# Attention block with a maximum brought in by a one-row product: the tile of that product, 64 rows against 32

## The chip, the cores and the metric

One core of a Trainium2 chip runs the whole program. The metric is the device time of one execution in microseconds. Five engines work beside each other and meet at semaphores: TensorE (PE, with its weight loads as PEld), VectorE (DVE), ScalarE (ACT), GpSimd (POOL) and SyncE (SP), which here issues the transfers.

## What is computed

The block takes `L0_attn_data`, 8 x 512 x 128 in float32, normalises each row, and returns the sum of three things: the input, a 16-head attention over the normalised rows, and a gated recurrence over them that ends in a tanh.

```
x = L0_attn_data                                   # (8, 512, 128)
xn = _layernorm(x, axis=-1)
# attention: 16 heads of 64
qkv = xn @ W_qkv + b_qkv
scores = jnp.einsum('nqhd,nkhd->nhqk', q, k)
attention = jax.nn.softmax(scores / jnp.sqrt(64.0), axis=3)
out = jnp.einsum('nhql,nlhd->nqhd', attention, v).reshape(n, l, 1024) @ W_out + b_out
# recurrence over the 8 entries of the first axis
ft = sigmoid(xt @ wf.T + c @ uf.T + bf); it = sigmoid(...); gt = tanh(...)
c = ft * c + it * gt
h = tanh(xn @ wo.T + c_final @ uo.T + bo)
return x + out + h
```

## The kernel before, in words

The work is written out by hand, one block of code for each engine, with semaphores between them; no scheduler reorders it. The outer loop runs over the 8 batches (the first and the last are written out, the six between are a loop), the loop inside over 4 steps `j` of a batch. A step handles two head pairs `t` and `t + 1`; there are 64 head pairs in all. A head pair is two heads of 64 features each, one in partitions 0 to 63 and one in partitions 64 to 127 (`OWN[0]` and `OWN[1]`).

For precision, queries and keys are split into a high and a low part (`QH`, `QL`, `KH`, `KL`), so a block of scores is the sum of three products. `scores` (line 786) makes the transposed scores of one block `u` of 128 keys against 512 queries for both heads, in PSUM tile `st[:, u % 2, h, :]`: line 796 accumulates KH·QH, KH·QL and KL·QH, each as a pair of products, one for each head, with 64 rows of the array each. The softmax needs the maximum of each query taken off before the exponential. `score_maxima` (line 770) computes rough scores the other way round in `mx`, VectorE reduces them to negated maxima (line 551, `NM`), `turn_max` (line 781) transposes them, and SyncE's transfers place them as single rows of `MROW` in partitions 0 and 64 (`AUX`, line 187). The fourth and last pair of `scores`, line 804, adds that row to every one of the 128 key rows: the stationary operand `ONEROW` has ones in partitions 0 and 64 and zeros elsewhere, and the moving operand `MROW` has the maxima there and zeros elsewhere (lines 236 to 241). This pair too is contracted over 64 rows for each head. The last product of the pair signals `st_done`, and ScalarE's exponential (line 387) takes the tile.

In between, the TensorE block issues other products in a fixed order: the next heads' projections (`pair_of_halves`, line 729, 64 rows each), the rough scores (line 777, 64 rows), the product of probabilities and values (line 812, 128 rows and 64 columns of the array), the sums of the probabilities (line 822, also 128 by 64), the output projection (line 828, 128 by 128), and in the first batch the projections of the first heads and the recurrence (lines 693 and 712, 128 by 128). How high a product's tile is follows from how many partitions its operands have, and where it stands from their first partition.

Of the kernel before, what the change touches and what calls it, by code (L numbers as in the profile page):

```python
# [5 lines left out]
def build_block(nc, data, W_qkv, b_qkv, W_out, b_out, wf, uf, bf, wi, ui, bi, wc, uc, bc, wo, uo, bo, in_c, out):  # L6
# [11 lines left out]
    HD = P // 2  # L18
# [7 lines left out]


    OWN = [slice(0, HD), slice(HD, P)]
    AUX = [slice(0, 1), slice(HD, HD + 1)]

    data_t = data.rearrange("n (b p) d -> p n b d", p=P)
# [4 lines left out]
    with ctx:  # L36
        def sb(name, shape, dt=f32):
            return ctx.enter_context(nc.sbuf_tensor(name, shape, dt))
# [22 lines left out]
        MROW = sb("MROW", [P, 2, L], f32r)  # L61
        ONEROW = sb("ONEROW", [P, P], f32r)
# [29 lines left out]
        st = ctx.enter_context(nc.psum_tensor("st", [P, 2, 2, L], f32))  # L92
# [53 lines left out]
        def wait(eng, s, value):  # L146

            if not (isinstance(value, int) and value <= 0):
                eng.wait_ge(s, value)

        def placed(n, j):

            return (STRETCHES * n + j + 1) * 32
# [11 lines left out]
        def _(sp):  # L165
# [16 lines left out]
            def place_max(n, j):  # L182
# [3 lines left out]
                for h in range(2):  # L186
                    sp.dma_start(MROW[AUX[h], :, :].bitcast(f32).rearrange("p a (b j) -> p (a b) j", j=P),
                                 TM[2 * TB * h:2 * TB * h + 2 * TB, :]).then_inc(d_m, 16)

            def place_first(a, copied, landed):  # L190
                sp.wait_ge(copied, 1)
                for h in range(2):
                    sp.dma_start(MROW[AUX[h], a, :].bitcast(f32).rearrange("p (b j) -> p b j", j=P),
                                 TM[2 * TB * h + TB * a:2 * TB * h + TB * (a + 1), :]).then_inc(landed, 16)
# [34 lines left out]
        def _(pool):  # L229
# [10 lines left out]
            for h in range(2):  # L240
                nc.gpsimd.memset(ONEROW[AUX[h], :].bitcast(f32), 1.0).then_inc(pads_set, 1)
                pool.wait_ge(pads_set, 3 + h)
# [446 lines left out]
        def _(pe):  # L689
# [32 lines left out]
            def pair_of_halves(groups, slots, halved, done):  # L722

                for slot in slots:
                    swap, i = slot // 3, slot % 3
                    for h in range(2):
                        dst, terms = groups[h ^ swap]
                        stationary, moving = terms[i]
                        last = nc.tensor.matmul(dst, stationary[OWN[h], :], moving[OWN[h], :], start=(slot == 0),  # L729
                                                stop=(slot == 5))  # L730
# [39 lines left out]
            def score_maxima(t, s, b):  # L770
# [5 lines left out]
                for h in range(2):  # L776
                    last = nc.tensor.matmul(mx[:, h, :], QH[OWN[h], s % 4, b * P:(b + 1) * P], KH[OWN[h], s % 4, :],  # L777
                                            start=True, stop=True)
# [7 lines left out]
            def scores(n, t, s, u, parts=range(4)):  # L786

                b = slice(u * P, (u + 1) * P)
                terms = ((KH, QH), (KH, QL), (KL, QH))
                if 0 in parts:  # L790
                    wait(pe, exp_done, 4 * t + u - 1)
                for i in parts:
                    if i < 3:
                        k, q = terms[i]
                        for h in range(2):
                            nc.tensor.matmul(st[:, u % 2, h, :], k[OWN[h], s % 4, b], q[OWN[h], s % 4, :],  # L796
                                             start=(i == 0), stop=False)
                    else:
                        if u == 0 and isinstance(n, int) and n == 0 and s < 2:
                            pe.wait_ge(d_m if s else d_first, 32)  # L800
                        elif u == 0 and s % 2 == 0:
                            pe.wait_ge(d_m, placed(n, s // 2))
                        for h in range(2):
                            last = nc.tensor.matmul(st[:, u % 2, h, :], ONEROW[OWN[h], :], MROW[OWN[h], s % 2, :],  # L804
                                                    start=False, stop=True)
                        last.then_inc(st_done, 1)

            def values(n, t, s, blocks=range(TB)):

                for kb in blocks:  # L810
                    for h in range(2):
                        last = nc.tensor.matmul(value_banks[s % 2][OWN[h], :],  # L812
                                                VALL[:, kb, s * P + h * HD:s * P + (h + 1) * HD],
# [4 lines left out]
            def sums(t, s, dst):  # L818

                pe.wait_ge(sum_done, t + 1)  # L820
                for h in range(2):
                    last = nc.tensor.matmul(dst[OWN[h], :], ones[:, :], PSUMK[:, s % 2, h, :], start=True, stop=True)  # L822
                last.then_inc(den_done, 1)
# [54 lines left out]
            for c in range(PAIRS):  # L878
                last = nc.tensor.matmul(pv[:, 0:1], WO[:, c, :], bcol[:, B_V + c:B_V + c + 1],
                                        start=(c == 0), stop=(c == PAIRS - 1))  # L880
# [17 lines left out]
            def step(n, first, last):  # L898
                for j in range(STRETCHES):
# [4 lines left out]
                    if first and j == 0:  # L904
                        pe.wait_ge(first_tm, 1)
                        score_maxima(1, 1, 0)
                        pe.wait_ge(q_lo, 1)
                        pe.wait_ge(k_lo, 1)
                        scores(0, 0, 0, 0, (0, 1, 2))
                        score_maxima(1, 1, 1)  # L910
                        pe.wait_ge(q_lo, 2)
                        pe.wait_ge(k_lo, 2)
                        scores(0, 0, 0, 1, (0, 1, 2))
                        scores(0, 0, 0, 0, (3,))
                        scores(0, 0, 0, 1, (3,))
                        pe.wait_ge(bias_fin, 1)
# [198 lines left out]
```

## Time and profile before

| | |
|---|---|
| median of 2 runs | 884.73 us (884.01 to 885.45) |
| the profiled execution | 886.38 us, its span 884.6 us |
| TensorE busy | 858.7 us (97%), 5431 products |
| weight loads | 544.7 us (62%), 5431 |
| VectorE, ScalarE, GpSimd busy | 561.9, 450.6, 569.9 us |
| mean granted clock of TensorE | 0.991 of 2.4 GHz |

Each product (MATMUL) in the trace has a weight load (LDWEIGHTS) of its own, shown on PEld. A shape such as 64*128 64x512 is 64 rows and 128 columns of the array, with a moving operand of 512 columns. Products are pipelined and their ends are modelled, so the time between starts says more than the duration of one. A row of the timeline with x2 is two products of one line that were merged because they run into each other.

### The profile page before, as it was taken

How to read it: one execution, taken by the hardware profiler on the slowest of the kernel's cores; microseconds unless marked ns; L12 is line 12 of the kernel's file. 1: busy time of each engine (PE TensorE's matmuls, PEld its weight loads, DVE VectorE, ACT ScalarE, POOL GpSimd, SP SyncE). 2: the span in 40 equal slices, each digit the busy share in tenths (PEclk: the TensorE clock that was granted, in tenths of full speed). 3: DMA queues.
4: the chain of work that ended last, by engine and by line, in shares of the span. 5: the costliest groups of instructions: out<-in, count | busy, mean ns of one | idle time of the engine just before them, and what ended most of it. 6: DMA issues, size and time to landing. Idle time of an engine off the chain costs nothing.

```text
span 884.6 us, 14964 instructions
## 1 busy us (share of the span) xinstructions
PE 858.7 (97%) x5431; PEld 544.7 (62%) x5431; DVE 561.9 (64%) x743; ACT 450.6 (51%) x585; POOL 569.9 (64%) x299
## 2 busy tenths in 40 slices
PE   6979999999999999999999999999999999999998
PEld 4646575566666566666666566666666566666553
DVE  6576765655776577755776577755776577765722
ACT  6446574554555255554555255554555255554530
POOL 4635685375777477775777477775777477775764
PEclk9899999999999999999999999999999999999999
DMA  8000000000100010000100010000100010000000
GB/s 238 1 1 1 25 1 1 13 1 1 38 1 13 0 36 0 7 5 0 36 0 13 0 36 0 7 5 0 36 0 12 0 36 0 12 1 1 13 13 12
DMA packets 18635, 13.75 MB, mean 16 GB/s; under 512 B 1298, under 2 KB 16176, under 8 KB 18608
## 3 DMA queue, kind: packets, MB, share of 16 engines
q1 hardware_dynamic: 18560, 13.37, 4.9%
q8 instruction: 17, 0.28, 0.1%
q14 instruction: 10, 0.08, 0.0%
q10 hardware_dynamic: 48, 0.02, 0.0%
HBM read 6.83 MB, written 2.10 MB: 10 GB/s over the span
## 4 chain that ended last, share of the span: by engine, by line
PE 92%; DVE 4%; ACT 2%; issue 1%; DMA 0%; POOL 0%
PE st L796 20%; PE pv L812 13%; PE misc L812 12%; PE st L729 9%; PE mx L777 8%; PE st L804 6%; PE mx L828 6%; PE mx L822 6%; PE misc L712 2%; PE pv L729 2%; PE misc L729 2%; DVE NM L551 2%; PE pv L712 1%; ACT probs L387 1%; PE mx L712 1%
## 5 line engine op out<-in xcount | busy, mean ns | idle before, releaser
L551 DVE TENSOR_REDUCE NM<-mx 128x2 f32<-128x1024 f32 x256 | 313.9, 1226 | 160.0 <-PE mx L777 159.8
L387 ACT ACTIVATE probs<-st 128x1024 f32<-128x1024 f32 x256 | 256.9, 1027 | 78.7 <-PE st L804 71.9
L272 POOL TENSOR_TENSOR AT<-AT,RD 128x512 f32<-128x512 f32 x63 | 80.8, 1282 | 203.6 <-DVE RD L569 145.4
L280 POOL TENSOR_TENSOR PSUMK<-probs 128x1024 f32<-128x1024 f32 x64 | 153.4, 2397 | 56.3 <-ACT probs L387 56.3
L286 POOL TENSOR_TENSOR PSUMK<-PSUMK,probs 128x1024 f32<-128x1024 f32 x64 | 152.9, 2389 | 6.3 <-ACT probs L387 0.4
L293 POOL TENSOR_TENSOR PSUMK<-PSUMK,probs 128x1024 f32<-128x1024 f32 x64 | 152.7, 2386 | 6.1
L812 PE MATMUL misc<-probs,VALL 128*64 128x512 f32 x512 | 129.4, 593 | 0.7 <-DVE DL L516 0.7
L812 PE MATMUL pv<-probs,VALL 128*64 128x512 f32 x512 | 126.4, 614 | 3.0 <-DVE RES L522 3.0
L777 PE MATMUL mx<-KH,QH 64*128 64x512 f32 x512 | 107.7, 415 | 6.8 <-DVE NM L551 5.7
L796 PE MATMUL st<-QH,KH 64*128 64x512 f32 x512 | 105.1, 405 | 0.6 <-ACT probs L387 0.6
L796 PE MATMUL st<-QL,KH 64*128 64x512 f32 x512 | 101.8, 392 | 0.0
L796 PE MATMUL st<-QH,KL 64*128 64x512 f32 x512 | 101.8, 392 | 0.0
L804 PE MATMUL st<-MROW,ONEROW 64*128 64x512 f32 x512 | 101.5, 392 | 0.0
L565 DVE STREAM_TRANSPOSE RD<-mx 128x512 f32<-128x512 f32 x63 | 45.1, 716 | 76.4 <-PE mx L822 76.4
L812 PEld LDWEIGHTS misc<-probs,VALL 128*64 128x64 f32 x512 | 65.2, 137 | 46.0 <-issue 8.8
L379 ACT COPY AT<-misc 128x512 f32<-128x512 f32 x31 | 18.2, 586 | 137.9 <-PE misc L812 137.8
L777 PEld LDWEIGHTS mx<-KH,QH 64*128 64x128 f32 x512 | 48.4, 184 | 62.6 <-issue 28.3
L379 ACT COPY AT<-pv 128x512 f32<-128x512 f32 x32 | 18.8, 587 | 132.7 <-PE pv L812 132.7
L822 PE MATMUL mx<-PSUMK,ones 128*64 128x512 f32 x252 | 73.9, 592 | 0.0
L812 PEld LDWEIGHTS pv<-probs,VALL 128*64 128x64 f32 x512 | 44.9, 139 | 45.4 <-issue 31.3
L796 PEld LDWEIGHTS st<-QH,KH 64*128 64x128 f32 x512 | 48.4, 185 | 36.3 <-ACT probs L387 29.8
L828 PE MATMUL mx<-AT,WO 128*128 128x512 f32 x128 | 56.5, 593 | 0.0
(175 smaller groups left out, 1236.0 us busy)
## 6 DMA issues: line engine op xcount, KB each, us to landing
XSH<-XH SPq DMA_DIRECT2D x8, 256.0 KB, 2.4
XSL<-XL SPq DMA_DIRECT2D x8, 256.0 KB, 2.4
RES<-in_L_attn_data_dram SPq DMA_DIRECT2D x8, 256.0 KB, 2.7
out_dram<-RES SPq DMA_DIRECT2D x8, 256.0 KB, 2.3
probs<-in_L_attn_W_qkv_dram SPq DMA_DIRECT2D x3, 512.0 KB, 5.5
AT<-in_L_attn_data_dram SPq DMA_DIRECT2D x2, 512.0 KB, 7.0
MROW<-TM SPq DMA_DIRECT2D x62, 4.0 KB
AT<-in_L_attn_data_dram SPq DMA_DIRECT2D x1, 768.0 KB, 8.1
```

The source lines that it names most:

```text
L280: nc.gpsimd.tensor_tensor(PSUMK[:, s % 2, :, :], e[:, :, 0, :], e[:, :, 1, :], ALU.add).then_inc(sum_part, 1)
L286: nc.gpsimd.tensor_tensor(PSUMK[:, s % 2, :, :], PSUMK[:, s % 2, :, :], probs[:, s % 2, :, 2, :], ALU.add).then_inc(sum_part, 1)
L293: nc.gpsimd.tensor_tensor(PSUMK[:, s % 2, :, :], PSUMK[:, s % 2, :, :], probs[:, s % 2, :, 3, :], ALU.add).then_inc(sum_done, 1)
L387: nc.scalar.activation(probs[:, s % 2, :, u, :], st[:, u % 2, :, :], ACT.Exp, scale=SCALE).then_inc(exp_done, 1)
L551: nc.vector.tensor_reduce(NM[:, 0:4 * TB].rearrange("p (h a b) -> p h a b", h=2, a=2)[:, :, s % 2, b], mx[:, :, :], AX.X, ALU.max, negate= ...
L729: last = nc.tensor.matmul(dst, stationary[OWN[h], :], moving[OWN[h], :], start=(slot == 0), stop=(slot == 5))
L777: last = nc.tensor.matmul(mx[:, h, :], QH[OWN[h], s % 4, b * P:(b + 1) * P], KH[OWN[h], s % 4, :], start=True, stop=True)
L796: nc.tensor.matmul(st[:, u % 2, h, :], k[OWN[h], s % 4, b], q[OWN[h], s % 4, :], start=(i == 0), stop=False)
L804: last = nc.tensor.matmul(st[:, u % 2, h, :], ONEROW[OWN[h], :], MROW[OWN[h], s % 2, :], start=False, stop=True)
L812: last = nc.tensor.matmul(value_banks[s % 2][OWN[h], :], VALL[:, kb, s * P + h * HD:s * P + (h + 1) * HD], probs[:, s % 2, h, kb, :], star ...
L822: last = nc.tensor.matmul(dst[OWN[h], :], ones[:, :], PSUMK[:, s % 2, h, :], start=True, stop=True)
L828: last = nc.tensor.matmul(dst, WO[:, c, :], AT[:, c, :], start=(c == 0), stop=(c == PAIRS - 1))
```

## The change

The stationary and the moving operand of line 804 are cut to 32 partitions for each head, 0 to 31 and 64 to 95. The rows with data, 0 and 64, are among them; the rows left out are the zeros of both operands. The program then gives these products a tile of 32 rows and 128 columns in place of 64 and 128, at the same first rows 0 and 64. All other products keep theirs. The number of instructions and their order on each engine are the same in both kernels; a new line above moves line 804 to 805.

```diff
     OWN = [slice(0, HD), slice(HD, P)]
+    QUARTER = [slice(0, 32), slice(HD, HD + 32)]
     AUX = [slice(0, 1), slice(HD, HD + 1)]
...
                         for h in range(2):
-                            last = nc.tensor.matmul(st[:, u % 2, h, :], ONEROW[OWN[h], :], MROW[OWN[h], s % 2, :],
+                            last = nc.tensor.matmul(st[:, u % 2, h, :], ONEROW[QUARTER[h], :], MROW[QUARTER[h], s % 2, :],
                                                     start=False, stop=True)
```

## Rows read from the trace of the kernel before

**Rows 1.** The page: busy time of each engine, and three of its costliest groups
```profile
PE 858.7 (97%) x5431; PEld 544.7 (62%) x5431; DVE 561.9 (64%) x743; ACT 450.6 (51%) x585; POOL 569.9 (64%) x299
...
L551 DVE TENSOR_REDUCE NM<-mx 128x2 f32<-128x1024 f32 x256 | 313.9, 1226 | 160.0 <-PE mx L777 159.8
L387 ACT ACTIVATE probs<-st 128x1024 f32<-128x1024 f32 x256 | 256.9, 1027 | 78.7 <-PE st L804 71.9
...
L804 PE MATMUL st<-MROW,ONEROW 64*128 64x512 f32 x512 | 101.5, 392 | 0.0
```
**Rows 2.** Windows: stretch, length, busy PE, PEld, DVE, ACT, POOL, then PEclk, DMA
```profile
255.00:360.00 105.00, 105.00 (x708) 68.61 (x708) 69.08 (x81) 55.41 (x70) 71.24 (x35) 1.00 0.03 11
```
**Rows 3.** The page: the chain that ended last, by engine
```profile
PE 92%; DVE 4%; ACT 2%; issue 1%; DMA 0%; POOL 0%
```
**Rows 4.** What TensorE's products waited for: us in total, times, longest
```profile
PE mx L777 <- DVE NM L551: 5.7, 8, 1.3
...
PE st L729 <- ACT probs L387: 1.2, 3, 0.4
```
**Rows 5.** Timeline of PE, batch 4: start us, us, line, out<-in, rows*columns
```profile
480.97 0.40 PE L804 MATMUL st<-MROW,ONEROW 64*128 64x512 f32 x2
...
481.67 0.39 PE L796 MATMUL st<-QH,KL 64*128 64x512 f32 x2
481.90 0.39 PE L804 MATMUL st<-MROW,ONEROW 64*128 64x512 f32 x2
482.13 0.40 PE L777 MATMUL mx<-KH,QH 64*128 64x512 f32 x2
```
**Rows 6.** Timeline of the weight loads there
```profile
481.67 0.19 PEld L804 LDWEIGHTS st<-MROW,ONEROW 64*128 64x128 f32 x2
```
**Rows 7.** Timeline of the weight loads, the transposition of 30 rows at the start
```profile
7.80 0.18 PEld L853 LDWEIGHTS misc<-ident,probs 30*128 30x128 f32 x1 [0.43 <-DMA probs<-in_L_ffn_in_c_dram]
```
**Rows 8.** Timeline of PE, from 64-row to 128-row products in batch 4
```profile
489.55 0.39 PE L777 MATMUL mx<-KH,QH 64*128 64x512 f32 x2
489.87 0.50 PE L712 MATMUL misc<-XH,gwH 128*128 x1
490.20 0.39 PE L712 MATMUL misc<-XH,gwL 128*128 x1
490.43 0.40 PE L712 MATMUL misc<-XL,gwH 128*128 x1
```
**Rows 9.** Timeline of the weight loads there
```profile
489.87 0.19 PEld L712 LDWEIGHTS misc<-XH,gwH 128*128 128x128 f32 x1 [0.26 <-issue]
```
**Rows 10.** Timeline of PE, line 804 before 128-row products; then a change of columns
```profile
33.58 0.40 PE L804 MATMUL st<-MROW,ONEROW 64*128 64x512 f32 x2
33.91 0.50 PE L693 MATMUL st<-XH,WH 128*128 128x512 f32 x1
34.24 0.40 PE L693 MATMUL st<-XH,WL 128*128 128x512 f32 x1
...
35.17 0.40 PE L693 MATMUL st<-XL,WH 128*128 128x512 f32 x1
35.50 0.43 PE L784 MATMUL mx<-ident,NM 128*64 128x128 f32 x2
```
**Rows 11.** Timeline of PE, from 128-row to 64-row products in the first batch
```profile
119.95 0.39 PE L712 MATMUL misc<-DL,gwH 128*128 128x512 f32 x1
120.27 0.50 PE L796 MATMUL st<-QH,KH 64*128 64x512 f32 x2
120.61 0.40 PE L796 MATMUL st<-QL,KH 64*128 64x512 f32 x2
```
**Rows 12.** Timeline of PE in the first batch, with waits [idle before <-releaser]
```profile
47.28 0.50 PE L777 MATMUL mx<-KH,QH 64*128 64x512 f32 x2 [1.08 <-DVE NM L551]
...
49.19 0.50 PE L777 MATMUL mx<-KH,QH 64*128 64x512 f32 x2 [0.49 <-DVE NM L551]
```
**Rows 13.** Windows, columns as in rows 2, the stretch around the first of these waits
```profile
45.00:48.00 3.00, 1.92 (x18) 1.28 (x16) 2.37 (x4) 2.05 (x2) 0.66 (x1) 1.00 0.00 0
```

## The prediction

> **What bounds the kernel now.** I read the busy shares first, then the chain that ended last, then the waits, then the order of time inside one batch. TensorE is busy for 97% of the span, the next engine for 64% [rows 1]; from 255 to 780 us its busy time fills each of five stretches of 105 us, one batch long, completely, at a granted clock of 1.00, the upper of its two levels (2.4 GHz) [rows 2]. 92% of the chain that ended last is TensorE's [rows 3]. TensorE's own waits for other engines are short; the two that can recur in every batch are 5.7 us in all for the reduction at line 551 and 1.2 us for the exponentials [rows 4]. The others wait for TensorE: the exponentials 71.9 us for line 804 alone, the reduction 159.8 us for line 777 [rows 1]. So time added between two of TensorE's products is time added at the end, except where it falls into one of these few waits.
>
> **How that stream runs.** Each score row is four pairs: three of line 796 and the one of line 804. The two products of a pair work on the two halves of the array's rows at the same time: they are 0.39 to 0.40 us long, yet the five pairs from 480.97 to 482.13 us take 1.16 us, 0.232 us a pair [rows 5]. This is possible because the weights of a pair are loaded while the pair before runs: the loads for line 804 stand at 481.67, where the last pair of line 796 starts, and the products of line 804 start at 481.90 [rows 5, 6].
>
> **What the change does, part by part.** It adds and removes no instruction, and the order on every engine stays. Line 804 has 512 products, 256 pairs [rows 1]. Their columns stay 512 and their weights' 128, so their own length should stay: products with 512 columns take 0.39 to 0.40 us with 64 rows and with 128, once their load lies ahead of them [rows 5, 8]. The rows dropped hold zeros. Cost of this part: nothing either way. What is new is that a pair with tiles of 32 rows stands between pairs with tiles of 64. The array goes to another tile before line 804 and back behind it.
>
> **The price of a change of tile.** The trace has no clean change from 64 to 32 rows. The only narrower tile, a transposition of 30 rows, comes behind a wait for a DMA [rows 7] and gives no price. The nearest rows are the changes between 64 and 128 rows. From 64 to 128: line 777 starts at 489.55, line 712 at 489.87, 490.20 and 490.43: 0.32, 0.33, then 0.23 again [rows 8]. The first wide load says why: it starts only at 489.87, not at 489.55 [rows 9], so nothing is loaded under the last narrow pair; and the first wide product, with its load open in front of it, is 0.50 us long in the records, so the second comes late as well. The same from line 804 itself to line 693: 33.58, 33.91, 34.24 [rows 10]. The way back, from 128 to 64: 119.95, 120.27, 120.61 [rows 11]. Two starts take 0.65, 0.66 and 0.66 us where two pairs of one tile take 0.464: a change costs 0.193 us on their mean. About 0.09 of it is the late first start, the rest the load that lies open.
>
> The bounds: below, nothing, if 64 and 32 rows count as one tile to the chip; above, the 0.20 just read. A gain has no source, since loads already lie under products and the beat is set by the columns. I take 0.193, because the changes read paid it alike in both directions.
>
> The Trainium skill, TensorEngine Tiling (Array Packing), section Tiling Modes, lists two-fold and four-fold row tiling as separate configurations and says that a change of mode, as against a change of tile within one, drains the engine. The trace agrees for 64 against 128 rows; for 32 no row here shows it. The page speaks of the drain alone: read to the letter, that is the late first start, 504 changes at 0.09 us or 45 us, where the rows with the open load give 97.
>
> **How many changes.** The 256 pairs stand in 255 runs (only two of the first stand together, lines 914 and 915). Each run follows a 64-row pair: 255 changes in. Behind six runs stands a 128-row product that pays a change already: line 918 behind line 915, line 925 behind line 923, the gates at line 973 in three steps of the first batch, and line 1041 once. So 249 changes out. Sum: 504 x 0.193 = 97.3 us.
>
> **What is given back.** Where TensorE waits already, the added time falls into the wait. Such a place: in the first batch line 777 waits 1.08 and 0.49 us for the reduction, a score row in front of each [rows 12]. Two changes, 0.39 us, fit into either, because that reduction is paced by the products of line 777 and not by line 804. The waits shown sum to 6.9 us [rows 4]; I take 4, with bounds of 0 and 7. The work that hides this is the reduction's 1226 ns [rows 1]; where it no longer ends last, the full 0.193 is paid. ScalarE's loop gains room: an exponential takes 1027 ns [rows 1], and the score row between two of one bank gets 0.39 us longer.
>
> Added: 97.3 - 4 = 93.3 us. The profiled execution took 886.4 us, of which 884.6 span; with the added time 979.7. The median of the runs shown is 1.65 us lower, so I forecast 978. With the bounds (504 x 0.185 - 7 = 86; 504 x 0.20 = 101) this case reaches from 971 to 986.
>
> **The rivals.**
> *No change of tile for the chip (the other side).* If only a change to the full height or of the columns needs the array empty, and going between a half and a quarter of the rows costs nothing, then nothing moves: 884.7. For it: no row shows this change; all those read go to or from 128 rows. Against it: from 128*128 to 128*64, where the rows stay and only the columns change, the start is as late (35.17 to 35.50 us) [rows 10], so it seems that any difference of shape costs. It decides up to a price of 0.035 us a change (504 x 0.035 = 17.6 us, 2%).
> *Half a price.* Only one direction pays (255 or 249 x 0.193 = 49 us), or the array empties but the load no longer lies open (504 x 0.09 = 45). With 4 given back: 926 to 930. For it: the two parts are separate in the rows. Against it: both parts stand in every change read.
> *The pair no longer runs together.* If two 32-row tiles at rows 0 and 64 go one after the other, each pair takes 0.232 us more, 256 x 0.232 = 59 us on top: 1037. Against it: they lie in different halves of the array, as before. The Trainium skill, TensorE: Matmul & The Clock Gate, Part 3, has tiles in different row groups running at once; the trace agrees for the halves (a pair every 0.232 us) [rows 5], and for quarters no row here shows it.
> *The clock.* Would the gaps lower it? It stays 1.00 from 45 to 48 us, where TensorE is busy for only 1.92 of 3.00 us [rows 13], with waits ten times as long as the gaps forecast here. No chance of its own.
>
> **How the numbers follow.** Full price 0.72, half price 0.11, no price 0.13, no longer together 0.04. The forecast is that of the first, 978 us; its own range is 971 to 986. The range given takes in half price, 922 to 988, and leaves out 0.17. About 2% is what a measurement of this kernel can tell from no change: slower 0.87 (all but the case without a price), same 0.13, and faster 0.00, raised to 0.01 at the cost of slower, for a mechanism I have not thought of.
>
> **What would show it.** Right: the load of line 804 (805 in the changed file) no longer at the start of the pair before, but some 0.32 us behind it; 0.32 us from the last pair of line 796 to line 804 and some 0.43 from there to the next pair, where both are 0.23 now; the products of line 804 about 0.50 us long in the records, like the first ones behind the changes read [rows 8, 10, 11]; a batch of 105 us near 117 (32 pairs, 64 changes); ScalarE's wait for line 804 longer, TensorE's for VectorE in the first batch shorter. Wrong: loads of line 804 still under the pair before (no price); a late start with a load that runs ahead (half price); the two products of a pair starting 0.2 us apart (not together); a granted clock under 1.00 in the middle of the kernel.

## The result

The changed kernel takes 978.76 us (978.14 to 979.38), against 884.73 before: a ratio of 1.1046, with an interval of 1.102 to 1.1072. The forecast was 978, with a range of 922 to 988.

| | before | changed |
|---|---|---|
| median of 2 runs, us | 884.73 | 978.76 |
| profiled execution and its span, us | 886.38, 884.6 | 978.14, 976.3 |
| TensorE busy | 858.7 (97%) | 953.2 (98%) |
| products and weight loads | 5431, 5431 | 5431, 5431 |
| changes of tile between one product and the next | 108 | 612 |
| mean granted clock | 0.991 | 0.992 |

The changes of tile are counted over all products of the two traces: 504 were added, the number of the prediction. The page of the changed kernel, with the columns of [rows 1, 3]; line 805 is line 804 of before, 797 is 796, 778 is 777, 552 is 551, 388 is 387 (in the experiments below the numbers shift by a few more; the operands name the products):

```profile
PE 953.2 (98%) x5431; PEld 542.0 (56%) x5431; DVE 561.7 (58%) x743; ACT 456.8 (47%) x585; POOL 568.6 (58%) x299
...
PE 94%; DVE 4%; ACT 1%; issue 0%; DMA 0%; POOL 0%; SPq 0%; POOLq 0%
...
L552 DVE TENSOR_REDUCE NM<-mx 128x2 f32<-128x1024 f32 x256 | 313.8, 1226 | 251.0 <-PE mx L778 250.8
L388 ACT ACTIVATE probs<-st 128x1024 f32<-128x1024 f32 x256 | 262.7, 1027 | 157.8 <-PE st L805 157.8
...
L805 PE MATMUL st<-MROW,ONEROW 32*128 32x512 f32 x512 | 127.6, 496 | 0.0
...
L805 PEld LDWEIGHTS st<-MROW,ONEROW 32*128 32x128 f32 x512 | 47.3, 182 | 93.2 <-issue 93.2
```

The other engines do the same work in nearly the same time (ScalarE is busy for 456.8 us where it was 450.6, VectorE for 561.7 and 561.9) and wait longer: ScalarE's exponentials 157.8 us for line 805 where it was 71.9, VectorE's reductions 250.8 where it was 159.8 [rows 1]. The products of line 805 are 496 ns long where they were 392. And the weight loads of line 805 have 93.2 us of idle time in front of them, charged to "issue", which means that nothing in the profile is seen to hold them. What holds them shows in the order of time. First the products of the changed kernel around the narrow pair of a score row, as in [rows 5]:

```profile
524.70 0.40 PE L797 MATMUL st<-QH,KL 64*128 64x512 f32 x2
525.03 0.50 PE L805 MATMUL st<-MROW,ONEROW 32*128 32x512 f32 x2
525.46 0.51 PE L797 MATMUL st<-QH,KH 64*128 64x512 f32 x2
525.80 0.40 PE L797 MATMUL st<-QL,KH 64*128 64x512 f32 x2
526.04 0.40 PE L797 MATMUL st<-QH,KL 64*128 64x512 f32 x2
```

Then the weight loads there, as in [rows 6]:

```profile
525.02 0.18 PEld L805 LDWEIGHTS st<-MROW,ONEROW 32*128 32x128 f32 x2 [0.36 <-issue]
525.46 0.18 PEld L797 LDWEIGHTS st<-QH,KH 64*128 64x128 f32 x2 [0.25 <-issue]
...
525.80 0.19 PEld L797 LDWEIGHTS st<-QH,KL 64*128 64x128 f32 x2
```

Read the second list against the first. The load of 525.80 stands where the pair before its own starts: it is hidden, and its products start at 526.04. The load of line 805 does not stand at 524.70, where it would have in the kernel before, but at 525.02, 0.32 us behind the start of the wide pair and with its own products, which are recorded from 525.03. The load at 525.46 stands 0.43 us behind the start of the narrow pair, again with its own products. (The ends of products are modelled, so the lists do not tell to a few hundredths whether the pair before is through by then.) From one wide pair to the next across the narrow one: 524.70, 525.03, 525.46, 525.80, so 0.33, 0.43 and 0.34 us where 0.232 was the beat each time, 0.40 us more for two changes.

The time by batches is read from where the output projection (line 828, 829 in the changed file) begins, once in each batch from the second on. In the kernel before, the first of these places and the last two:

```profile
192.87 0.59 PE L828 MATMUL mx<-AT,WO 128*128 128x512 f32 x1
...
789.89 0.59 PE L828 MATMUL mx<-AT,WO 128*128 128x512 f32 x1
863.62 0.59 PE L828 MATMUL mx<-AT,WO 128*128 128x512 f32 x1
```

The same three places of the changed kernel:

```profile
201.21 0.59 PE L829 MATMUL mx<-AT,WO 128*128 128x512 f32 x1
...
873.54 0.59 PE L829 MATMUL mx<-AT,WO 128*128 128x512 f32 x1
955.41 0.59 PE L829 MATMUL mx<-AT,WO 128*128 128x512 f32 x1
```

| stretch | before, us | changed, us | added | changes added | us a change |
|---|---|---|---|---|---|
| to the first of these places | 192.87 | 201.21 | 8.3 | 73 | 0.11 |
| six batches | 597.02 | 672.33 | 75.3 | 384 | 0.196 |
| to the last place | 73.73 | 81.87 | 8.1 | 47 | 0.17 |
| the tail | 20.9 | 20.9 | 0.0 | 0 | |

In the full batches next to nothing comes back: 0.196 is nearly the 0.20 that the starts above give for each of two changes. What comes back does so at the start, and a little at the end.

### The profile page after: what moved, and what is told of

Its sections match the earlier page's. It is cut to its first block, busy times and chain, and to the rows that moved or that the text cites. A ratio compares the mean times of both kernels' runs of the same rounds, so it can differ in the third digit from the quotient of the medians.

```text
span 976.3 us, 14964 instructions
## 1 busy us (share of the span) xinstructions
PE 953.2 (98%) x5431; PEld 542.0 (56%) x5431; DVE 561.7 (58%) x743; ACT 456.8 (47%) x585; POOL 568.6 (58%) x299
## 4 chain that ended last, share of the span: by engine, by line
PE 94%; DVE 4%; ACT 1%; issue 0%; DMA 0%; POOL 0%; SPq 0%; POOLq 0%
PE st L797 21%; PE pv L813 12%; PE misc L813 11%; PE st L805 11%; PE mx L778 9%; PE st L730 8%; PE mx L829 6%; PE mx L823 5%; PE misc L730 3%; PE pv L730 2%; PE misc L713 2%; DVE NM L552 2%; PE pv L713 1%; PE mx L713 1%; PE st L694 1%
## 5 line engine op out<-in xcount | busy, mean ns | idle before, releaser
L552 DVE TENSOR_REDUCE NM<-mx 128x2 f32<-128x1024 f32 x256 | 313.8, 1226 | 251.0 <-PE mx L778 250.8
L388 ACT ACTIVATE probs<-st 128x1024 f32<-128x1024 f32 x256 | 262.7, 1027 | 157.8 <-PE st L805 157.8
L805 PE MATMUL st<-MROW,ONEROW 32*128 32x512 f32 x512 | 127.6, 496 | 0.0
L778 PE MATMUL mx<-KH,QH 64*128 64x512 f32 x512 | 115.5, 448 | 5.7 <-DVE NM L552 5.1
L797 PE MATMUL st<-QH,KH 64*128 64x512 f32 x512 | 115.0, 446 | 0.0
L805 PEld LDWEIGHTS st<-MROW,ONEROW 32*128 32x128 f32 x512 | 47.3, 182 | 93.2 <-issue 93.2
```

What stands on the lines that cost most here:

```text
L388: nc.scalar.activation(probs[:, s % 2, :, u, :], st[:, u % 2, :, :], ACT.Exp, scale=SCALE).then_inc(exp_done, 1)
L552: nc.vector.tensor_reduce(NM[:, 0:4 * TB].rearrange("p (h a b) -> p h a b", h=2, a=2)[:, :, s % 2, b], mx[:, :, :], AX.X, ALU.max, negate= ...
L805: last = nc.tensor.matmul(st[:, u % 2, h, :], ONEROW[QUARTER[h], :], MROW[QUARTER[h], s % 2, :], start=False, stop=True)
```

## The experiments

The theory: every change of the tile's shape costs TensorE some 0.2 us, whatever the product. Against it stand three others: that the narrow product itself is slow; that the program as a whole runs slower once a narrow tile is in it; that it matters which rows of the array the narrow tiles lie on.

**Narrow tiles in every second score row.**

```diff
+                        rows = QUARTER if u % 2 else OWN
                         for h in range(2):
-                            last = nc.tensor.matmul(st[:, u % 2, h, :], ONEROW[QUARTER[h], :], MROW[QUARTER[h], s % 2, :],
+                            last = nc.tensor.matmul(st[:, u % 2, h, :], ONEROW[rows[h], :], MROW[rows[h], s % 2, :],
```

> Narrow tiles of 32 rows for the odd score rows alone, 64 rows for the even ones. Changes of tile: 128 in, 122 out (six odd runs have a 128-row product behind them, where a change stood before), 250 in all. If each change costs 0.193 us: 250 x 0.193 = 48 us, less some 2 us that fall into waits, 884.7 + 46 = 931 us (928 to 934). If the added time came from something that is there once the narrow tile is used at all (a lower clock, a mode of the whole program): near 979. In the trace even rows should keep 0.23 us between the last pair of the three and the one behind it.

Measured: 927.98 us, a ratio of 1.0461 (1.0444 to 1.0479) to the kernel before, which took 887.27 us beside it. So 40.7 us were added where narrow tiles in every row add 91.0 on the same chip (978.24, the run with both tiles in one half, below): a little under half, and 5 us less than the 46 I expected. The trace holds 250 added changes, as counted. Its products, one wide and one narrow row:

```profile
496.79 0.40 PE L797 MATMUL st<-QH,KL 64*128 64x512 f32 x2
497.02 0.39 PE L806 MATMUL st<-MROW,ONEROW 64*128 64x512 f32 x2
497.25 0.40 PE L797 MATMUL st<-QH,KH 64*128 64x512 f32 x2
...
497.71 0.39 PE L797 MATMUL st<-QH,KL 64*128 64x512 f32 x2
498.03 0.50 PE L806 MATMUL st<-MROW,ONEROW 32*128 32x512 f32 x2
498.46 0.50 PE L778 MATMUL mx<-KH,QH 64*128 64x512 f32 x2
```

Around the wide pair the beat stays 0.23; around the narrow one it is 0.32 and 0.43. So the price is local and the program as a whole is not slowed. By batches, the beginnings of the output projection stand at 512.58 and 617.88 us:

```profile
512.58 1.46 PE L830 MATMUL mx<-AT,WO 128*128 128x512 f32 x3
...
617.88 1.03 PE L830 MATMUL mx<-AT,WO 128*128 128x512 f32 x2
```

A batch takes 105.3 us, 5.8 more than before, for 32 changes: 0.181 each, a little under the 0.196 of the full change. Nor does the missing part all sit in the first batch, as it does there. By the trace this half microsecond in a batch does not lie at the changes, whose starts are as late as in the full change. It lies mostly in the beat of the wide pairs, which between the fourth and the fifth output projection follow each other every 0.2297 us on the mean where nothing holds them, against 0.2315 in the kernel before and 0.2324 in the changed kernel. What sets that beat stays open.

**A second narrow pair behind the first, and the same with wide ones.** Both add a pair of products with a stationary operand of zeros to each score row, in one case to the changed kernel, in the other to the kernel before.

```diff
+        ZROW = sb("ZROW", [P, P], f32r)
...
                         for h in range(2):
                             last = nc.tensor.matmul(st[:, u % 2, h, :], ONEROW[QUARTER[h], :], MROW[QUARTER[h], s % 2, :],
-                                                    start=False, stop=True)
+                                                    start=False, stop=False)
+                        for h in range(2):
+                            last = nc.tensor.matmul(st[:, u % 2, h, :], ZROW[QUARTER[h], :], MROW[QUARTER[h], s % 2, :],
+                                                    start=False, stop=True)
```

(ZROW is set to zero at the start, in lines left out here. In the second kernel OWN stands for QUARTER.)

> The changed kernel with a second narrow pair right behind the first, on the same 32 rows, whose stationary operand is all zeros, so that it adds nothing. Changes of tile stay 504, narrow pairs double to 512. If the price is one of the change, the second pair costs what any pair costs, 0.232 us: 978.8 + 256 x 0.232 = 1038 us (1034 to 1041), and its load stands under the first pair. If the price sits in the narrow pair itself (0.39 us more than a wide one): 978.8 + 256 x 0.62 = 1138 us.

> The kernel before with the same second pair of zeros behind line 804, in tiles of 64 rows. No change of tile is added. 884.7 + 256 x 0.232 = 944 us (940 to 946), where waits take nothing. The difference to the run with two narrow pairs should then again be that between the two kernels, 94 us; if the narrow pair itself were slow, twice that.

Measured: with two narrow pairs 1036.5 us, ratio 1.1672 (1.1644 to 1.17); with two wide pairs 936.59 us, ratio 1.0561 (1.0539 to 1.0582), on the same chip. The products of the first of these kernels:

```profile
557.08 0.40 PE L799 MATMUL st<-QH,KL 64*128 64x512 f32 x2
557.41 0.50 PE L807 MATMUL st<-MROW,ONEROW 32*128 32x512 f32 x2
557.75 0.40 PE L810 MATMUL st<-MROW,ZROW 32*128 32x512 f32 x2
558.07 0.50 PE L799 MATMUL st<-QH,KH 64*128 64x512 f32 x2
558.41 0.40 PE L799 MATMUL st<-QL,KH 64*128 64x512 f32 x2
```

And their weight loads:

```profile
557.41 0.18 PEld L807 LDWEIGHTS st<-MROW,ONEROW 32*128 32x128 f32 x2 [0.37 <-issue]
557.51 0.19 PEld L810 LDWEIGHTS st<-MROW,ZROW 32*128 32x128 f32 x2
558.07 0.18 PEld L799 LDWEIGHTS st<-QH,KH 64*128 64x128 f32 x2 [0.37 <-issue]
```

The second narrow pair's load stands at 557.51, under the first pair and on the same rows as it: loads run ahead for narrow tiles as for wide ones. The second pair is 0.40 us long, as wide ones are; only the first is 0.50. It starts 0.34 behind the first instead of 0.23, because of the first one's open load, and the way out then shows its late start alone: 0.32, and 0.34 once more. Here the two parts of the price lie apart: some 0.09 us of late start and some 0.11 behind it, where the load lies open, on the way in and on the way out. The whole second pair costs 1036.5 - 978.2 = 58.3 us, 0.228 for each of 256, taking the 978.24 us of the next kernel as the changed kernel's time on this chip. By batches it is 0.233 (the output projections of this kernel are 119.5 us apart, those of the changed kernel 112.05 on the mean). A narrow product is no slower than a wide one, and a narrow pair does run together.

In the kernel before, the added wide pair follows at the plain beat:

```profile
502.34 0.39 PE L806 MATMUL st<-MROW,ONEROW 64*128 64x512 f32 x2
502.57 0.40 PE L809 MATMUL st<-MROW,ZROW 64*128 64x512 f32 x2
```

It added 49.3 us in place of the 59 expected. Some of that was taken back at the start, as with the change itself: the first output projection begins 3.2 us later (196.04 for 192.87 us), behind 40 of the 256 pairs, 9.3 us at the full price. A batch (from 515.45 to 621.92 us) is 7.0 us longer for 32 pairs, 0.218 a pair, so again about 0.4 us of a batch is missing, and again it lies in the beat of the wide pairs, 0.2301 us on the mean here. The run with two narrow pairs is 1036.5 - 936.59 = 99.9 us longer, where the two kernels without the second pair differ by 91.0 on this chip: more by about what the wide pairs fell short.

**The narrow tiles in one half of the array.** The second head's row of maxima goes to partition 32 in place of 64.

```diff
-    QUARTER = [slice(0, 32), slice(HD, HD + 32)]
-    AUX = [slice(0, 1), slice(HD, HD + 1)]
+    QUARTER = [slice(0, 32), slice(32, HD)]
+    AUX = [slice(0, 1), slice(32, 33)]
```

> The changed kernel with the second head's row of maxima in partition 32 in place of 64, so that the two narrow tiles lie side by side in the lower half of the array. If tiles of 32 rows run together wherever they lie: 979 us, as the changed kernel (976 to 982). If only tiles in different halves do: 0.232 us more for each pair, 978.8 + 59 = 1038 us. If the price of the change depended on which rows the narrow tiles share with the wide ones, another time than both.

Measured: 978.24 us, ratio 1.1024 (1.1005 to 1.1042) to the 887.27 us of the kernel before beside it, against 1.1046 (1.102 to 1.1072) for the changed kernel. Whether the two narrow tiles lie in one half or in both makes no difference here, neither to their running together nor to the price:

```profile
525.67 0.40 PE L797 MATMUL st<-QH,KL 64*128 64x512 f32 x2
526.00 0.50 PE L805 MATMUL st<-MROW,ONEROW 32*128 32x512 f32 x2
526.42 0.50 PE L797 MATMUL st<-QH,KH 64*128 64x512 f32 x2
526.76 0.40 PE L797 MATMUL st<-QL,KH 64*128 64x512 f32 x2
```

**The other way: 128 rows.** From the kernel before, line 804 is contracted over all rows, with one stationary operand for each head: ONEROW keeps its ones in row 0 alone, ONELOW has ones in row 64 (the lines that set them are left out).

```diff
+        ONELOW = sb("ONELOW", [P, P], f32r)
...
                         for h in range(2):
-                            last = nc.tensor.matmul(st[:, u % 2, h, :], ONEROW[OWN[h], :], MROW[OWN[h], s % 2, :],
+                            last = nc.tensor.matmul(st[:, u % 2, h, :], (ONELOW if h else ONEROW)[:, :], MROW[:, s % 2, :],
                                                     start=False, stop=True)
```

> The kernel before with line 804 contracted over all 128 rows for each head (one stationary operand with ones in row 0, one with ones in row 64), so tiles of 128 rows and no pair. If any change of tile costs the same: some 498 added changes (the six runs with a 128-row product behind them now lose their change) x 0.193 = 96 us, and the two products one after the other, 256 x 0.232 = 59 us; less 4: 885 + 151 = 1036 us (1030 to 1042). If a change to 32 rows were dearer or cheaper than one to 128 rows by a half, the changed kernel and this one would differ in their added time by some 45 us beside those 59.

Measured: 1037.1 us, ratio 1.1686 (1.1658 to 1.1714) to 887.52 us. The trace holds 606 changes, 498 more than before.

```profile
557.25 0.39 PE L799 MATMUL st<-QH,KL 64*128 64x512 f32 x2
557.56 0.50 PE L807 MATMUL st<-MROW,ONEROW 128*128 128x512 f32 x1
557.90 0.40 PE L807 MATMUL st<-MROW,ONELOW 128*128 128x512 f32 x1
558.23 0.50 PE L780 MATMUL mx<-KH,QH 64*128 64x512 f32 x2
```

These starts are 0.31, 0.34 and 0.33 us apart; with two narrow pairs they were 0.33, 0.34 and 0.32. By batches, two output projections that stand at 569.46 and 689.24 us are 119.8 us apart, 20.3 more than before; less 32 beats of 0.232 for the products that no longer run together, 64 changes cost 12.9 us, 0.20 each. A change from 64 to 128 rows, the one that the trace of before showed, costs what a change from 64 to 32 costs, which it did not show. That was the step of the prediction with no row under it.

What was not tried: four narrow tiles at work at once, a pair of zeros on rows 32 to 63 and 96 to 127 beside the first one. They would add into the same two blocks of PSUM as the first pair at the same time, and the kernel's other PSUM tiles are in use. So whether four tiles would earn back their two changes stays open. I saw no version faster than the kernel before in these runs: what they show is a price, and no run changes the tile less often than the kernel before.

## Why the prediction was right

*What bounds the kernel.* As read: TensorE is busy for 98% and the added time went into the end, while the other engines waited longer.

*No change in the product itself.* Right. The second narrow pair is 0.40 us long and costs 0.228.

*The price of a change.* I took 0.193 us from changes between 64 and 128 rows, for a change between 64 and 32 that no row showed. The six full batches give 75.3 / 384 = 0.196. The 128-row experiment shows that it was fair to carry it over. The two parts, 0.09 for the late start and the rest for the open load, lie apart in the run with two narrow pairs. "Half a price" and "no change of tile for the chip" are out by the loads at 525.02 and 525.46, which stand with their own products and no longer at the start of the pair before. The late start alone, forecast at 45 us, falls short by half of the 91.7 added: behind it a load lies open. The Trainium skill, TensorEngine Tiling (Array Packing), section Tiling Modes, lists row tiling in tiles of 32 rows as a separate configuration and says that a change of mode drains the engine, without a price; the rows here agree that a change between 64 and 32 rows is paid for. "No longer together" is out by the 0.228 us for a pair.

*The number of changes.* 504 forecast, 504 in the trace.

*The clock.* Right: the granted clock is 1.00 in every stretch of 100 or 117 us from 60 to 862 us of the changed kernel, narrow tiles or not.

*What is given back.* Here the step was mis-sized. I took 4 us with a bound of 7, read from the list of waits. By the profiles, at the price of the full batches, it is 504 x 0.196 = 98.8 less 91.7 added to the span: 7.1 us, just over the bound. And most of it does not come out of that list, whose two entries of 6.9 us [rows 4] are still 5.8 in the changed kernel.

The direct waits took the changes in as told. TensorE's waits for line 551 at 47.28 and 49.19 us before [rows 12], with a third,

```profile
51.01 0.50 PE L777 MATMUL mx<-KH,QH 64*128 64x512 f32 x2 [0.39 <-DVE NM L551]
```

are these in the changed kernel:

```profile
49.35 0.49 PE L778 MATMUL mx<-KH,QH 64*128 64x512 f32 x2 [0.46 <-DVE NM L552]
...
51.26 0.50 PE L778 MATMUL mx<-KH,QH 64*128 64x512 f32 x2 [0.29 <-DVE NM L552]
...
53.08 0.50 PE L778 MATMUL mx<-KH,QH 64*128 64x512 f32 x2 [0.19 <-DVE NM L552]
```

From one of these products to the next it is 1.91 and 1.82 us, as before, so two changes, 0.39 us, were taken in whole each time. (The idle times shrink by less, 0.20, because the narrow pair in front is 0.1 us longer in the records and starts 0.09 later.) With the first wait the three took in some 1.5 us.

Of the 6.0 us that came back before 201 us (73 x 0.196 less 8.3), most stands in waits too short for the list of [rows 4], which counts a wait only where TensorE is seen idle. The weight loads show them. Loads of line 777 waited for the reduction 24 times before, and 9 times in the changed kernel:

```profile
PEld mx L777 <- DVE NM L551: 12.8, 24, 1.6
...
PEld mx L778 <- DVE NM L552: 8.1, 9, 1.6
```

In the kernel before, such a load was held by line 551 until 77.87 us:

```profile
77.87 0.18 PEld L777 LDWEIGHTS mx<-KH,QH 64*128 64x128 f32 x2 [0.37 <-DVE NM L551]
```

It then lay open in front of its product, and two beats were 0.33 us long though no wait is listed:

```profile
77.55 0.39 PE L796 MATMUL st<-QL,KH 64*128 64x512 f32 x2
77.88 0.50 PE L777 MATMUL mx<-KH,QH 64*128 64x512 f32 x2
78.21 0.39 PE L796 MATMUL st<-QH,KL 64*128 64x512 f32 x2
```

The same place in the changed kernel, where line 552 was done in time, has the plain beat:

```profile
78.44 0.39 PE L797 MATMUL st<-QL,KH 64*128 64x512 f32 x2
78.67 0.39 PE L778 MATMUL mx<-KH,QH 64*128 64x512 f32 x2
78.90 0.39 PE L797 MATMUL st<-QH,KL 64*128 64x512 f32 x2
```

That is 0.20 us back at one place. Set against each other product by product, with 0.196 us taken off for each change, the two lists have some 20 such steps between 73 and 201 us of the changed kernel, 4.4 us in all; a few of them are loads that ScalarE's exponentials had held. A last part, some 1.3 us, is the clock. In both kernels TensorE had waited 2.8 us for line 522 (523) and was at work again; from 65 to 70 us the granted clock was 0.78 before, a mixture of its two levels (1.2 and 2.4 GHz), and 1.00 in the changed kernel. The kernel with both tiles in one half had 0.77 there and came to the first output projection 1.1 us later (202.35 in place of 201.21 us), while the kernel with two wide pairs had 1.00. So this part does not follow the size of the tile. What decides it from one execution to the next, these single profiles don't show. Up to 33 us, in turn, the changed kernel had lost some 1.6 us beside the price of its changes, part of it at a lower granted clock (0.75 from 30 to 35 us, where it was 1.00 before).

So the price and the count were right by the mechanism, and the sum came out as close as it did by luck: 97.3 less 4 were forecast, 98.8 less 7.1 measured, 93.3 against 91.7, with a slightly low price and too little given back. That the median is closer still, 978.76 to 978, is chance: the medians of the runs scatter by about a microsecond around the profiled executions.

*A slip in reading.* I called a stretch of 105 us one batch. A batch is 99.5 us, by the starts of the output projection, and is now 112.0; the added 12.5 was forecast as 12.4, on the wrong base (117).

## What to carry to other kernels

Before giving one product in a dense stream another tile, count how often the shape of the tile changes from one product to the next: each change, in either direction, between 64 and 32 rows as between 64 and 128, cost about 0.2 us here, close to a whole pair of products with 512 columns. A smaller tile brought nothing by itself where the columns stayed, so match the tile of the neighbours and fill the unused rows with zeros. The mark in a profile is a weight load that starts with its own product and not at the start of the one before, idle time before it charged to "issue", and a first product that is 0.50 us long where its neighbours have 0.40.

## What the runs showed that I had not expected

A short wait costs more than the profile's list of waits says. A load that comes late by a little leaves itself open in front of its product, and the next start is late as well; the list calls TensorE busy all the while. This is why more came back than the list held.

The beat of the pairs is not quite constant from kernel to kernel. The batches of the kernels with every second row narrow and with two wide pairs were 0.4 to 0.5 us shorter than the price of their parts, since wide pairs followed each other there every 0.230 us in place of 0.2315. So an added wide pair cost 0.218 us, while the second narrow pair cost its full share. What sets this stays open.
